# Delta rule in chunks: block-diagonal 128-row products for the inverse's halves and the updates, keys and queries in one product of 128 columns, v turned by VectorE and ScalarE

## The chip, the cores and the metric

One core of one Trainium2 chip runs the whole program in one launch. The metric is device time in microseconds (us); lower is better. TensorE is called PE in the profile (PEld is its weight load), VectorE DVE, ScalarE ACT, GpSimd POOL, SyncE SP.

## The reference, cut to what matters

The program is two layers of a network over 4096 tokens of 256 values. The change touches one of their four parts, the gated delta rule of the first layer: 16 heads of 64 channels, and for each head a 64 x 64 state S that is carried through all 4096 tokens.

```python
def step(S, inp):
    q_t, k_t, v_t, g_t, b_t = inp
    Sk = jnp.einsum('bhkv,bhk->bhv', S, k_t)
    delta = jnp.einsum('bhv,bhk->bhkv', v_t, k_t) - jnp.einsum('bhv,bhk->bhkv', Sk, k_t)
    S = jnp.exp(g_t)[..., None, None] * S + b_t[..., None, None] * delta
    o_t = jnp.einsum('bhkv,bhk->bhv', S, q_t)
    return (S, o_t)
```

## The kernel before, in words

The stages follow one another: norm and router, projections with a short convolution (`phase_projections`), the delta rule (`phase_delta`), the experts, a second norm, and an attention of 8 heads that takes the second half of the time. Only `phase_delta` changes. All of its data are float32.

**Chunks and couples.** `phase_delta` cuts the tokens into 64 chunks of C = 64. Two chunks make a couple; there are 32 couples (L754 to L780). The 16 heads are NPAIR = 8 pairs: the two heads of a pair lie on partitions 0 to 63 and 64 to 127, so every tile is 128 partitions x 8 pairs x 64. Within a chunk the recurrence becomes matrix work: a 64 x 64 triangular matrix of each head (`upper`, from keys times keys, decays and beta) is inverted by doubling, and the inverse times a residual gives the updates `u`, which go into the outputs and the new state.

**Quarter products.** Every product of a pair and head is a matmul of 64 rows, 64 weight columns and 64 moving columns (`product`, L835), so each uses one quarter of the 128 x 128 array. SAME writes the half of the partitions from which it reads, OTHER the other half. `over_heads` (L976) issues 16 of them (8 pairs, 2 heads), or 32 when a SAME and an OTHER product go side by side; I call such an issue a **group**. The trace shows every float32 matmul as two records on PE and two weight loads on PEld.

**The inverse.** Levels k = 1 to 5 each do, for both chunks x of the couple: `half` (L905, `pd_pre` <- `inv_low`, `upper`) on TensorE, `mask_step` (L1251, `step`) on VectorE, `up` (L916, `pd_low` <- `inv`, `step`) on TensorE, `turn_low` (L1262, `inv_low`) on VectorE and `keep_inverse` (L1159, `inv`) on ScalarE, and after level 5 `keep_last_inverse` (L1165, `inv_fin`). Halves and ups are SAME.

**The rest of a couple**, for each x: keys with keys (`keys_keys`, L863), keys with queries (L877), keys by rows (L888), v by rows (`values`, L897: a product with minus the identity that starts the sum of the residual), residual (L923), old outputs (L933), updates (L944), new outputs (L951), new state (L962), and a projection of both chunks' outputs in two parts (`project`, L965, 128 rows by 64 columns, L972). ScalarE copies the residual out of PSUM (L1154).

**Order.** `couples(one)` (L774) writes the program of each engine out in full, without a loop, 34 times: `one(post, pre, ahead)` weaves three couples: `post` runs the recurrent part, `pre` is inverted, `ahead` has its keys and decays prepared. The order in each engine's `one` is by hand (TensorE L986, ScalarE L1176, VectorE L1266, GpSimd L1378, loads on SP L796), and semaphores tie them. On TensorE a couple is 26 steps: 24 groups and the projection's two parts.

Of the kernel before, what the change touches and what calls it, by code (L numbers as in the profile page):

```python
# [49 lines left out]
def shape_constants():  # L50
# [14 lines left out]
    for n in range(LEVELS):  # L65
# [7 lines left out]
        "less_eye": -eye_c,  # L73
# [609 lines left out]
def phase_delta(nc, g, ctx):  # L683
# [5 lines left out]
    def ps(name):  # L689
        return ctx.enter_context(nc.psum_tensor(name, [P, NPAIR, C], F32))  # L690
# [7 lines left out]
    def sem2(name):  # L698
# [7 lines left out]
    k_t, q_t, v_t = (sb(n, [P, 2, NPAIR, 2, C]) for n in ("k_t", "q_t", "v_t"))  # L706
# [3 lines left out]
    grow = sb("grow", [P, 4, NPAIR, C + 1])  # L710
    rel = sb("rel", [P, 4, NPAIR, C + 1])
    upper = sb("upper", [P, 4, NPAIR, C])
    k_g = sb("k_g", [P, 2, NPAIR, C])
# [5 lines left out]
    inv_fin = [sb(f"inv_fin{x}", W) for x in range(2)]  # L719
# [5 lines left out]
    o_t = sb("o_t", [P, 2, NPAIR, C])  # L725
# [5 lines left out]
    p_r, p_o, p_u, p_n = ps("pd_r"), ps("pd_o"), ps("pd_u"), ps("pd_n")  # L731
# [6 lines left out]
    val_d, res_d, ress_d, w_d, u_d, o_d, ocp_d = (sem(s) for s in ("val", "res", "ress", "w", "u", "o", "ocp"))  # L738
# [3 lines left out]
    kk_d, qk_d, kr_d, rows_d, upper_d, minus_d, att_d, inv1_d = (  # L742
        sem2(s) for s in ("kk", "qk", "kr", "rows", "upper", "minus", "att", "inv1"))
# [8 lines left out]

    SAME, OTHER = range(2)

# [28 lines left out]
    def _(sp):  # L783
# [12 lines left out]
        def one(post, pre, ahead):  # L796
# [10 lines left out]
            load("k", k_t, ahead).then_inc(k_in[ahead.odd], 16)  # L807
            if ahead.c == 0:
                sp.dma_start(wo[:], g.given["wo_t"].rearrange("(n p) d -> p n d", p=P)).then_inc(wo_in, 16)
# [4 lines left out]
            if ahead.c > 1:  # L814
                sp.wait_ge(val_d, ahead.ended[1] - 4)
# [4 lines left out]
            if ahead.c > 1:  # L820
                sp.wait_ge(o_d, ahead.ended[1] - 4)
            load("q", q_t, ahead).then_inc(q_in[ahead.odd], 16)
# [6 lines left out]
    def _(pe):  # L829
        te = nc.tensor  # L830

        def rows_of(half):
            return slice(half * C, (half + 1) * C)

        def product(p, h, out, to, lhs, rhs, start=True, stop=True, shared=False):  # L835
            return te.matmul(out[rows_of(h if to == SAME else 1 - h), p, :], lhs(p, rows_of(h)), rhs(p, rows_of(h)), start=start, stop=stop,  # L836
                             skip_group_check=shared)
# [12 lines left out]
        def wait_keys(n, x):  # L850
            pe.wait_ge(k_in[n.odd], n.filled)
            if x == 0:
                if n.c > 1:
                    pe.wait_ge(ress_d, n.ended[1] - 4)
                elif n.c > 0:
                    pe.wait_ge(upper_d[0], n.last)
            else:
                if n.c > 1:
                    pe.wait_ge(state_d, n.ended[1] - 3)
                if n.c > 0:  # L860
                    pe.wait_ge(att_d[1], n.last)

        def keys_keys(n, x):  # L863
# [3 lines left out]
        def wait_queries(n, x):  # L867
            pe.wait_ge(q_in[n.odd], n.filled)
            if x == 0:
                pe.wait_ge(upper_d[1], n.now)  # L870
                pe.wait_ge(rows_d[1], n.last)
            else:
                pe.wait_ge(att_d[0], n.now)
                if n.c > 0:
                    pe.wait_ge(state_d, n.ended[0] - 1)

        def keys_queries(n, x):  # L877
            return lambda p, h: product(p, h, p_n, OTHER, of_couple(k_t, n.ring[x]), of_couple(q_t, n.ring[x]))

        def wait_key_rows(n, x, ahead):  # L880
            if x == 0:
                pe.wait_ge(ocp_d, n.begun[0])
            elif ahead is not None:
                pe.wait_ge(upper_d[1], ahead.now)
            else:
                pe.wait_ge(state_d, n.ended[0])

        def key_rows(n, x):  # L888
            return lambda p, h: product(p, h, p_o if x == 0 else p_n, OTHER, of_couple(k_t, n.ring[x]), of_const("eye_c"))

        def wait_values(n, x, ahead):
# [1733 lines left out]
```

## Time and profile before

| | us |
|---|---|
| median of 3 runs (lowest to highest) | 4342.76 (4340.51 to 4347.18) |
| the profiled execution, its own time | 4350.06 |
| its span, first to last instruction | 4348.3 |
| TensorE busy, whole span | 3834.0 |
| VectorE busy, whole span | 2981.2 |
| delta stage, from the 1st to the 31st of the 32 couples' ends | 619.5 to 1827.4 |

The profiled execution's own time is the one that a sum over its rows has to be held against; the median of the runs is 7.3 us below it. Busy time on TensorE counts each matmul to its modelled end, so a matmul that took 0.22 us to come out of the array counts 0.22 us even where the next one started 0.03 us after it. "Idle before <- issue" is time in which the engine stood still and no semaphore of another engine explains it.

### The profile page before, as it was taken

The numbers are of one execution on the slowest core, as the hardware profiler recorded it, in microseconds if no ns is written. First come the engines' busy times: TensorE is split into PE (matmuls) and PEld (weight loads), VectorE is DVE, ScalarE is ACT, GpSimd is POOL, SyncE is SP. The second block draws the span as 40 slices with busy tenths as digits, with TensorE's granted clock in tenths as the row PEclk, the third lists the DMA queues.
The fourth block names the chain that finished last, engine by engine and source line by source line (L and its number), as shares of the span: only waits on it lengthen the run. The fifth ranks groups of instructions, "written<-read, shape, count | busy, mean of one in ns | idle before, by whom it ended". The sixth has DMA issues, their size and how long they took to land. (4 is left out here: it accounts for less than half of the span.)

```text
span 4348.3 us, 135609 instructions
## 1 busy us (share of the span) xinstructions
PE 3834.0 (88%) x56333; PEld 2258.0 (52%) x56333; DVE 2981.2 (69%) x4999; ACT 2057.0 (47%) x2941; POOL 1035.6 (24%) x1042
## 2 busy tenths in 40 slices
PE   5999777777777777799687999999999999999998
PEld 4444366666676666667465344444444444444443
DVE  5799754444454444444797787887878787878786
ACT  2788622222222222225343365665656565656554
POOL 1000055445554545300777200000000000000000
PEclk9999899999999999999898899999999999999999
DMA  3543532222222222135344100000000000000000
GB/s 125 183 126 116 158 102 77 85 77 74 84 78 78 79 77 80 37 96 154 112 109 121 38 5 8 15 10 14 10 14 3 19 5 19 5 9 13 10 14 10
DMA packets 271832, 265.83 MB, mean 61 GB/s; under 512 B 53761, under 2 KB 232065, under 8 KB 270497
## 3 DMA queue, kind: packets, MB, share of 16 engines
q1 hardware_dynamic: 250768, 226.11, 17.4%
q0 software_dynamic: 6144, 16.79, 1.2%
q10 hardware_dynamic: 14352, 14.55, 1.0%
q8 instruction: 457, 7.49, 0.7%
q14 instruction: 111, 0.90, 0.1%
HBM read 151.99 MB, written 105.38 MB: 59 GB/s over the span
## 5 line engine op out<-in xcount | busy, mean ns | idle before, releaser
L2411 DVE TENSOR_REDUCE part_max<-p_m 128x1 f32<-128x512 f32 x2118 | 1362.9, 685 | 378.5 <-PE p_m L2253 371.0
L2393 ACT ACTIVATE prob<-p_s 128x1024 f32<-128x1024 f32 x1024 | 1048.6, 1024 | 747.4 <-PE p_s L2317 745.5
L2272 PE MATMUL p_o<-prob,v_one 128*64 128x512 f32 x4096 | 1055.0, 592 | 3.9 <-ACT prob L2393 0.5
L2253 PE MATMUL p_m<-keys,queries 96*64 96x512 f16 x4236 | 662.0, 387 | 27.9 <-DMA keys<-parts_d 20.3
L2317 PE MATMUL p_s<-queries,keys 97*64 97x512 f16 x4096 | 619.6, 380 | 0.0
L2317 PEld LDWEIGHTS p_s<-queries,keys 97*64 97x64 f16 x4096 | 229.4, 109 | 597.1 <-issue 592.0
L836 PE MATMUL pd_pre<-inv_low,upper 64*64 64x64 f32 x10240 | 386.6, 226 | 97.3 <-issue 80.4
L2221 POOL TENSOR_TENSOR attn<-o_num,o_inv 32x512 f32<-32x512 f32 x64 | 81.0, 1266 | 1458.5 <-DVE o_inv L2430 1452.0
L836 PEld LDWEIGHTS pd_pre<-inv_low,upper 64*64 64x64 f32 x10240 | 351.6, 140 | 104.3 <-issue 92.8
L2253 PEld LDWEIGHTS p_m<-keys,queries 96*64 96x64 f16 x4236 | 239.4, 108 | 309.3 <-DVE part_max L2411 56.4
L1255 DVE TENSOR_TENSOR step<-pd_pre,const 128x512 f32<-128x512 f32 x320 | 218.9, 689 | 245.5 <-PE pd_pre L836 240.3
L836 PE MATMUL pd_low<-inv,step 64*64 64x64 f32 x8192 | 313.6, 226 | 83.5 <-issue 70.1
L2272 PEld LDWEIGHTS p_o<-prob,v_one 128*64 128x64 f32 x4096 | 289.1, 136 | 162.2 <-issue 15.9
L589 PE MATMUL p_proj<-xn_t_all,proj_w_sb 128*128 128x512 f32 x768 | 337.2, 595 | 7.7 <-PEq L2556 7.7
L1264 DVE STREAM_TRANSPOSE inv_low<-pd_low 128x512 f32<-128x512 f32 x256 | 182.3, 712 | 233.1 <-PE pd_low L836 229.9
L836 PEld LDWEIGHTS pd_low<-inv,step 64*64 64x64 f32 x8192 | 284.5, 140 | 83.8 <-issue 82.0
L1163 ACT ACTIVATE inv<-pd_low 128x512 f32<-128x512 f32 x192 | 114.6, 597 | 336.4 <-DVE inv_low L1264 333.0
L589 PEld LDWEIGHTS p_proj<-xn_t_all,proj_w_sb 128*128 128x128 f32 x768 | 146.6, 191 | 192.6 <-issue 187.3
L1163 ACT ACTIVATE inv_half<-pd_low 128x512 f32<-128x512 f32 x64 | 38.3, 598 | 262.9 <-DVE inv_low L1264 262.9
L972 PE MATMUL pd_u<-wo,o_t 128*64 128x256 f32 x1024 | 138.7, 415 | 4.2 <-issue 4.2
L2430 DVE RECIPROCAL o_inv<-o_raw 128x64 f32<-128x64 f32 x256 | 137.8, 540 | 0.0
L658 DVE SCALAR_TENSOR_TENSOR conv_k<-raw,conv_w_sb,conv_k 128x2048 f32<-128x2048 f32 x48 | 112.2, 2351 | 22.9 <-ACT raw L632 21.8
(244 smaller groups left out, 5837.1 us busy)
## 6 DMA issues: line engine op xcount, KB each, us to landing
q_d<-conv_q SPq DMA_DIRECT2D x16, 1024.0 KB, 5.0
v_d<-conv_v SPq DMA_DIRECT2D x16, 1024.0 KB, 5.0
k_d<-conv_k SPq DMA_DIRECT2D x16, 1024.0 KB, 6.5
sums<-sums_d SPq DMA_DIRECT2D x128, 128.0 KB, 3.8
k_t<-k_d SPq DMA_DIRECT2D x32, 512.0 KB, 4.1
sums_k<-sums_d SPq DMA_DIRECT2D x128, 128.0 KB, 3.0
v_t<-v_d SPq DMA_DIRECT2D x32, 512.0 KB, 4.6
q_t<-q_d SPq DMA_DIRECT2D x32, 512.0 KB, 5.2
```

Source lines behind the costliest of these rows:

```text
L589: last = te.matmul(p_proj[u % RING][:], g.proj_w_sb[:, n, c, p * P:(p + 1) * P], g.xn_t[:, c, b * BLK:(b + 1) * BLK], start=c == 0, stop=c ...
L836: return te.matmul(out[rows_of(h if to == SAME else 1 - h), p, :], lhs(p, rows_of(h)), rhs(p, rows_of(h)), start=start, stop=stop, skip_gr ...
L972: last = te.matmul(out[x * C:(x + 1) * C, 0:D], o_t[:, x, p, :], wo[:, p, :], start=p == 0, stop=p == NPAIR - 1)
L1163: a.activation(inv_half[x][:] if k == NL - 1 else inv[x][:], p_low[x][:], ACT.Copy).then_inc(up_d[x], 1)
L1255: v.tensor_tensor(step[x][:], p_pre[x][:], over_pairs(masks[:, k - 1, :]), ALU.mult).then_inc(step_d[x], 1)
L1264: v.transpose(inv_low[x][:], p_low[x][:]).then_inc(lowc_d[x], 1)
L2253: last = te.matmul(p_m[k % 2][x * HALF:(x + 1) * HALF, :], queries[0:ROW, p, hh, at:at + HALF], keys[0:ROW, 2 * p + hh, kb * BLK:(kb + 1) ...
L2272: product = te.matmul(p_o[64 * hh:64 * hh + VW, :], g.v_one[:, j, p, hh:hh + 2, :].rearrange("p a d -> p (a d)"), prob[:, j % 2, hh, :], s ...
L2317: last = te.matmul(p_s[j % 2][x * HALF:(x + 1) * HALF, hh, :], keys[0:KR, 2 * p + hh, at:at + HALF], queries[0:KR, p, hh, :], start=True, ...
L2393: a.activation(prob[:, j % 2], p_s[j % 2][:], ACT.Exp, scale=SCORE_SCALE).then_inc(exp_d, 1)
L2411: v.tensor_reduce(part_max[:, hh * SUB + sub, kb:kb + 1], p_m[k % 2][:], AX.X, ALU.max).then_inc(red_d, 1)
L2430: v.reciprocal(o_inv[:, i * PW:(i + 1) * PW], o_raw[:, i * PW:(i + 1) * PW]).then_inc(inv_d, 1)
```

## The change

`half` and `updates` become matmuls of 128 rows, 128 weight columns and 64 moving columns, one for a pair instead of two for its heads. To that end `upper` is copied into a zeroed block-diagonal tile `upper_wide` (`widen`, on ScalarE), and the last inverse is copied in two halves into a zeroed block-diagonal `inv_fin`. Keys with keys and keys with queries become one product with 128 moving columns (`keys`, `pd_kq` of two banks), and q is loaded earlier. The product `values` goes: VectorE turns v in 32 x 32 blocks (`turn_values`), ScalarE puts the blocks in place by eight copies for each chunk (`keep_values`, `v_row`), and VectorE subtracts the residual product from it (`residual`), which takes ScalarE's copy of the residual away. The projection becomes 128 x 128 weights for both chunks. The order of all engines is written anew.

```diff
-    k_t, q_t, v_t = (sb(n, [P, 2, NPAIR, 2, C]) for n in ("k_t", "q_t", "v_t"))
+    kq_t = sb("kq_t", [P, 2, 2, NPAIR, 2, C])
+    k_t, q_t = kq_t[:, 0], kq_t[:, 1]
+    upper_wide = sb("upper_wide", [P, 2, NPAIR, 2 * C])
+    inv_fin = [sb(f"inv_fin{x}", [P, NPAIR, 2 * C]) for x in range(2)]
...
+        def keys(n, x):
             key = of_couple(k_t, n.ring[x])
-            return lambda p, h: product(p, h, p_r if x == 0 else p_n, OTHER, key, key)
+            return lambda p, h: product(p, h, p_kq, OTHER, key, lambda p, hs: kq_t[hs, :, n.odd, p, x, :])
...
         def half(n, x):
-            return lambda p, h: product(p, h, p_pre[x], SAME, of(upper, n.ring[x]), of(inv_low[x]))
+            for p in range(NPAIR):
+                last = te.matmul(p_pre[x][:, p, :], upper_wide[:, x, p, :], inv_low[x][:, p, :], start=True, stop=True)
+            return last
...
         def updates(n, x):
-            return lambda p, h: product(p, h, p_u, SAME, of(inv_fin[x]), of(resid))
+            for p in range(NPAIR):
+                last = te.matmul(p_u[:, p, :], inv_fin[x][:, p, :], resid[:, p, :], start=True, stop=True)
+            return last
...
             for p in pairs:
-                for x in range(2):
-                    last = te.matmul(out[x * C:(x + 1) * C, 0:D], o_t[:, x, p, :], wo[:, p, :], start=p == 0, stop=p == NPAIR - 1)
+                last = te.matmul(out[:, 0:D], o_t[:, p].rearrange("p x t -> p (x t)"), wo[:, p, :], start=p == 0, stop=p == NPAIR - 1)
...
+        def keep_values(n, x, h):
+            for from_p, from_t, to_p, to_t in blocks_of(h):
+                last = a.activation(v_row[to_p, x, :, to_t], v_turned[from_p, :, from_t], ACT.Copy)
...
+        def widen(n, x):
+            if n.c > 0:
+                act.wait_ge(half_d[x], n.level[0])
+            act.wait_ge(minus_d[x], n.now)
+            for h in range(2):
+                last = a.activation(upper_wide[half_of(h), x, :, half_of(h)], upper[x][half_of(h)], ACT.Copy)
+            last.then_inc(wide_d[x], 1)
...
+        def turn_values(n, x):
+            v.transpose(v_turned[:], v_t[:, n.odd, :, x, :]).then_inc(vt_d[x], 1)
+
+        def residual(n, x):
+            v.tensor_tensor(resid[:], v_row[:, x], p_r, ALU.subtract).then_inc(ress_d, 1)
...
+        po.memset(upper_wide[:], 0.0).then_inc(cleared, 1)
+        for x in range(2):
+            po.memset(inv_fin[x][:], 0.0).then_inc(cleared, 1)
```

TensorE's order for one couple is now, with x after the point and "+" for products side by side: residual.0 + old.0; half.0, half.1 of level 1; updates.0; up.0; up.1 + new state.0; half.0, half.1 of level 2; up.0 + residual.1; up.1 + outputs.0; half.0 of level 3; updates.1; half.1 of level 3; old.1 + new state.1; up.0 + outputs.1; up.1 + keys.0 of the next couple but one; half.0, half.1 of level 4; up.0 + key rows.0; projection, first part; up.1 + keys.1; half.0, half.1 of level 5; projection, second part; up.0 + key rows.1; up.1.

Three places show what stands on TensorE. In an order's row, "64x64" or "128x64" is output partitions by moving columns, and xN a row repeated. The first is the end of a couple, level 5 and the second part of the projection (`pd_u<-wo,o_t`), before:

```order
L836 MATMUL pd_pre<-inv_low,upper 64x64 [waits d_lowc0]
L836 MATMUL pd_pre<-inv_low,upper 64x64 x15
L836 MATMUL pd_pre<-inv_low,upper 64x64 [waits d_lowc1]
L836 MATMUL pd_pre<-inv_low,upper 64x64 x15
L972 MATMUL pd_u<-wo,o_t 64x256 x8
```

and in the changed kernel:

```order
L901 MATMUL pd_pre<-inv_low,upper_wide 128x64 [waits d_lowc0]
L901 MATMUL pd_pre<-inv_low,upper_wide 128x64 x7
L901 MATMUL pd_pre<-inv_low,upper_wide 128x64 [waits d_lowc1]
L901 MATMUL pd_pre<-inv_low,upper_wide 128x64 x7
L977 MATMUL pd_u<-wo,o_t 128x256 x4
```

Each half has 8 matmuls instead of 16, and each part of the projection 4 instead of 8. The second is the middle of a couple, on TensorE at level 3, where the updates of chunk 1 stand, before:

```order
L836 MATMUL pd_o<-q_t,state 64x64 x15
L836 MATMUL pd_u<-resid,inv_fin 64x64 [waits d_u,d_ress,d_up1]
L836 MATMUL pd_u<-resid,inv_fin 64x64 x15
L836 MATMUL pd_pre<-inv_low,upper 64x64 [waits d_lowc0]
L836 MATMUL pd_pre<-inv_low,upper 64x64 x15
```

and in the changed kernel:

```order
L901 MATMUL pd_pre<-inv_low,upper_wide 128x64 x7
L948 MATMUL pd_u<-resid,inv_fin 128x64 [waits d_u,d_ress,d_up1]
L948 MATMUL pd_u<-resid,inv_fin 128x64 x7
L901 MATMUL pd_pre<-inv_low,upper_wide 128x64 [waits d_lowc1]
L901 MATMUL pd_pre<-inv_low,upper_wide 128x64 x7
```

The updates now stand between the two halves of level 3, and the old outputs, which stood alone in a group, have moved behind them to the side of the new state. Over the 32 couples TensorE has 14592 matmuls in this stage, before 19968: 456 for a couple instead of 624.

## Rows read from the trace of the kernel before

**Rows 1.** The page, first line and busy times: us (share of the span) x instructions.
```profile
span 4348.3 us, 135609 instructions
...
PE 3834.0 (88%) x56333; PEld 2258.0 (52%) x56333; DVE 2981.2 (69%) x4999; ACT 2057.0 (47%) x2941; POOL 1035.6 (24%) x1042
```

**Rows 2.** Windows, stretch, busy us of PE, PEld, DVE, ACT, POOL; clock, DMA share, GB/s.
```profile
1000.00:1400.00 400.00, 309.09 (x12380) 273.95 (x12380) 196.13 (x299) 105.95 (x188) 201.24 (x189) 0.96 0.25 80
```

**Rows 3.** Tile attn_tok, written once per couple: ns, first and last start.
```profile
L1204 ACT ACTIVATE attn_tok<-pd_u x31: 384/384/386, 619.5 to 1827.4; 128x256 f32<-128x256 f32 x31
```

**Rows 4.** Timeline, TensorE: start us, us, tiles, count [idle <- cause].
```profile
1199.79 0.22 PE L836 MATMUL pd_n<-q_t,k_t 64*64 64x64 f32 x1
...
1200.69 0.22 PE L836 MATMUL pd_n<-q_t,k_t 64*64 64x64 f32 x1
1200.73 1.11 PE L836 MATMUL pd_o<-q_t,state 64*64 64x64 f32 x32
1201.66 1.11 PE L836 MATMUL pd_u<-resid,inv_fin 64*64 64x64 f32 x32
...
1203.44 0.33 PE L836 MATMUL pd_pre<-inv_low,upper 64*64 64x64 f32 x5 [0.45 <-issue]
```

**Rows 5.** Waits of 1000 to 1400 us, TensorE: us in total, times, longest us.
```profile
PE pd_pre L836 <- issue: 28.8, 20, 3.2
...
PE pd_low L836 <- DVE step L1255: 2.9, 5, 0.6
```

**Rows 6.** DMA queues of 1000 to 1400 us: packets, MB, share.
```profile
q8 instruction: 98, 1.61, 1.7%
```

**Rows 7.** DMA queues of 110 to 510 us, the projections.
```profile
q8 instruction: 7, 0.11, 0.1%
```

**Rows 8.** Timeline, TensorE, half of a projection between two other groups.
```profile
1212.05 0.22 PE L836 MATMUL pd_o<-const,k_t 64*64 64x64 f32 x1
1212.19 1.95 PE L972 MATMUL pd_u<-wo,o_t 128*64 128x256 f32 x16
1214.07 0.27 PE L836 MATMUL pd_low<-inv,step 64*64 64x64 f32 x1
```

**Rows 9.** Timeline, TensorE, first group of the router product L451.
```profile
14.59 3.62 PE L451 MATMUL p_logits<-lin_w,xn_t 128*128 128x48 f32 x16 [0.87 <-ACT xn_t L401]
```

**Rows 10.** Windows over that group: stretch, busy us, clock, DMA share, GB/s.
```profile
14.60:18.10 3.50, 3.50 (x16) 3.45 (x16) 0.00 (x0) 0.67 (x3) 2.32 (x3) 1.00 1.11 338
2110.00:2112.00 2.00, 1.96 (x18) 1.76 (x16) 1.79 (x8) 0.94 (x2) 0.54 (x2) 1.00 0.00 0
```

**Rows 11.** Groups by form: transpositions by 128 columns, early and late.
```profile
L443 PE MATMUL p_xt<-const,xn 128*128 128x128 f32 x64 | 15.7, 427 | 16.6 <-DVE xn L264 16.6
...
L1826 PE MATMUL ps_xn<-const,xn 128*128 128x128 f32 x64 | 12.5, 278 | 24.5 <-DVE xn L1973 24.5
```

**Rows 12.** Timeline, TensorE, a group of L1861.
```profile
2110.01 1.95 PE L1861 MATMUL ps_qk<-z_t,qk_w 128*128 128x128 f32 x16
```

**Rows 13.** Groups by form, weight loads: busy us, mean ns.
```profile
L836 PEld LDWEIGHTS pd_pre<-inv_low,upper 64*64 64x64 f32 x10240 | 351.6, 140 | 104.3 <-issue 92.8 <-DVE inv_low L1264 6.5
...
L1861 PEld LDWEIGHTS ps_qk<-z_t,qk_w 128*128 128x128 f32 x512 | 59.8, 192 | 0.1
...
L451 PEld LDWEIGHTS p_logits<-lin_w,xn_t 128*128 128x128 f32 x128 | 27.9, 330 | 21.3 <-issue 21.3
```

**Rows 14.** Groups by form, 1000 to 1400 us: DVE and ACT.
```profile
L1255 DVE TENSOR_TENSOR step<-pd_pre,const 128x512 f32<-128x512 f32 x100 | 68.4, 688 | 80.1 <-PE pd_pre L836 78.4
L1264 DVE STREAM_TRANSPOSE inv_low<-pd_low 128x512 f32<-128x512 f32 x79 | 56.2, 712 | 75.0 <-PE pd_low L836 74.0
...
L1204 ACT ACTIVATE attn_tok<-pd_u 128x256 f32<-128x256 f32 x10 | 3.8, 384 | 29.6 <-PE pd_u L972 29.6
```

**Rows 15.** Timeline, VectorE, waiting for a product of TensorE.
```profile
1201.10 0.69 DVE L1238 TENSOR_TENSOR qk<-pd_n,rel 128x512 f32<-128x512 f32 x1 [0.38 <-PE pd_n L836]
```

**Rows 16.** Timeline, GpSimd, at the start of the delta stage.
```profile
535.56 1.83 POOL L1318 MEMSET rel<- 128x2080 f32 x1
```

More of the change, by code:

```diff
@@ L807, in one @@
             load("k", k_t, ahead).then_inc(k_in[ahead.odd], 16)
+            if ahead.c > 1:
+                for x in range(2):
+                    sp.wait_ge(kq_d[x], ahead.before)
+                    sp.wait_ge(qg_d[x], ahead.before)
+            load("q", q_t, ahead).then_inc(q_in[ahead.odd], 16)
             if ahead.c == 0:
@@ L814, in one @@
             if ahead.c > 1:
-                sp.wait_ge(val_d, ahead.ended[1] - 4)
+                for x in range(2):
+                    sp.wait_ge(vt_d[x], ahead.before)
             load("v", v_t, ahead).then_inc(v_in[ahead.odd], 16)
@@ L1080, in one @@
             if post is not None:
-                new.then_inc(new_d, 1)
+                out.then_inc(o_d, 1)
             if pre is not None:
@@ L1196, in one @@
             if post is not None:
+                keep_outputs(post, 0)
+            if pre is not None:
+                keep_inverse(pre, 0, 3)
+            if post is not None:
                 keep_outputs(post, 1)
             if pre is not None:
-                for k in (3, 4):
-                    for x in range(2):
-                        keep_inverse(pre, x, k)
+                keep_values(pre, 0, 0)
+                keep_inverse(pre, 1, 3)
+                keep_values(pre, 0, 1)
+                keep_inverse(pre, 0, 4)
+                keep_values(pre, 1, 0)
+                keep_inverse(pre, 1, 4)
+                keep_values(pre, 1, 1)
+            if ahead is not None:
+                for x in range(2):
+                    widen(ahead, x)
             if post is not None:
@@ L1266, in one @@
         def one(post, pre, ahead):
+            if post is not None:
+                residual(post, 0)
             if pre is not None:
@@ L1308, in one @@
             if ahead is not None:
+                attention(ahead, 1)
                 turn_first(ahead, 0)
+            if pre is not None:
+                take_rows(pre, 1)
+            if ahead is not None:
                 turn_first(ahead, 1)
@@ L1383, in one @@
                     decays(ahead, x)
-            if pre is not None:
-                grow_queries(pre, 0)
-                grow_keys(pre, 0)
-            if ahead is not None:
-                for x in range(2):
-                    scale_rel(ahead, x)
+                scale_rel(ahead, 0)
             if post is not None:
@@ L1396, in one @@
                 scatter(post)
+            if pre is not None:
+                grow_queries(pre, 1)
             if ahead is not None:
-                for x in range(2):
-                    minus_eye(ahead, x)
-                for x in range(2):
-                    first_inverse(ahead, x)
+                minus_eye(ahead, 0)
+                first_inverse(ahead, 0)
+                minus_eye(ahead, 1)
+                first_inverse(ahead, 1)
         couples(one)
```

359 lines of the change are left out of this document (172 added, 187 removed).

## The prediction

> **What bounds the kernel now.** The page first: TensorE is busy for 3834.0 us of 4348.3, and it is the only engine near the span [rows 1]. Then the windows, because only one stage changes. In 400 us of the delta stage TensorE is busy for 309.09 us, VectorE 196.13, ScalarE 105.95, GpSimd 201.24, at a granted clock of 0.96 [rows 2]. So TensorE leads here too, with a quarter of its time idle. The period comes from the tile that ends each couple: 31 writes, 619.5 to 1827.4 us [rows 3], 30 intervals of 40.26 us.
>
> What a group costs is in the timeline. A group of one product (32 records) starts at 1200.73 and the next at 1201.66: 0.93 us [rows 4]. A group of two products side by side, 64 records, spans 1199.79 to 1200.73 and takes no longer [rows 4]. So the price is 0.058 us for each of 16 turns, whether two or four quarters of the array work in it. The 24 groups of a couple are 22.3 us. Half a projection takes 16 records in 1.73 us (1.95 less the 0.22 until a result is out) [rows 8], two make 3.5. A change between the two tilings costs something: the last quarter matmul starts at 1212.05, the projection at 1212.19, where a quarter matmul would have followed after 0.03; I take 0.15 us for each of the four changes, 0.6. Together 26.4 us of the 40.26; TensorE stands still for nearly 14.
>
> The waits say why: "issue" ended 28.8 us of idle time before `pd_pre` alone, the VectorE step only 2.9 us before `pd_low` [rows 5]. A gap of 0.45 us stands in the middle of a group, at 1203.44, where no semaphore is asked [rows 4]. The DMA rows tell what it is: in 400 us of this stage the instruction queue brought 98 packets of 16.4 KB [rows 6], in 400 us of the projections 7 [rows 7]. TensorE ran 12380 + 12380 instructions in those 400 us [rows 2], so a packet holds 253 and one comes every 4.08 us. A couple's 624 matmuls are 2496 instructions, with some 30 waits 9.98 packets, 40.7 us: the stage moves at the pace at which TensorE's straight-line code is brought, not at the pace of the array.
>
> **The change, part by part (us per couple).**
>
> *Code.* 456 matmuls are 1824 instructions, with the waits 7.3 packets: 30.0 us at 4.08. This bound falls by 10.3.
>
> *Halves and updates.* Twelve groups of 16 records with 128 weight columns and 64 moving columns replace twelve of 32. Is the weight load the price? The nearest rows: L451 has 128 weight columns and 48 moving ones, and 16 records take 3.62 us [rows 9], (3.62 - 0.41) / 15 = 214 ns each, though 48 moving columns are fewer than here; early in the kernel everything is slow by a factor of two in spacing (the same transposition takes 427 ns there and 278 at L1826 [rows 11]), so I read it as the lower level of 1.2 GHz, against the 1.00 that the windows print for it [rows 10]. Half of 214 is 107 at 2.4 GHz. L1861, with 128 weight and 128 moving columns, takes (1.95 - 0.28) / 15 = 112 ns [rows 12]. The load's own record grows from 140 ns for 64 columns to 192 for 128, and to 330 early [rows 13], which fits a load of two cycles for a column that hides the matmul behind it. Bounds: 58 ns (a quarter matmul's turn) and 112; I take 110, next to the rows with 128 weight columns. A half is then 16 x 0.110 = 1.76 instead of 0.93, and it is alone, since the whole array is taken. Ten halves 17.6, two updates 3.5. The Trainium skill has the rule in "TensorE: Matmul & The Clock Gate", section "LDWEIGHTS (loading the stationary operand)": the time goes with the columns of the weights alone, columns / 1.2 ns. This gives 107 ns at either clock; the rows agree at the higher level and have twice that early. By it twelve groups would cost 0.6 less and the forecast would be 4365.
>
> *Keys and queries.* Two products of 128 moving columns, each beside an up: 16 x 0.110 = 1.76, two are 3.5. Key rows go beside ups.
>
> *The other groups* (two old outputs, two residuals, two outputs, two new states, ten ups, two key rows; two of the ups are with the keys above): ten groups of 0.93, 9.3.
>
> *Projection.* 16 records of 256 columns, 216 ns each (1.73 / 8, where two went side by side [rows 8]): 3.5, as before.
>
> *Changes of tiling.* Twelve instead of four, at 0.17 (0.14 seen, and a first load that is now longer): 2.0. Bounds 0.1 and 0.3. The Trainium skill, "TensorEngine Tiling (Array Packing)", "Key Properties", says that a change of tiling mode drains TensorE. Read strictly, each would cost the full 0.22 us of a result and the load, 0.3: 1.6 more for a couple, 4434 in all; the 0.14 us row speaks for a partial drain.
>
> Sum: 17.6 + 3.5 + 3.5 + 9.3 + 3.5 + 2.0 = 39.4, before 26.4. The array's work now exceeds the code's 30.0 and becomes the bound.
>
> *Waits that stay.* A mask takes 0.69, a turn 0.71 [rows 14], and VectorE starts 0.15 to 0.2 after the product's end [rows 15]: from the end of a group to the start of what needs it is 1.1 us. A half of 1.76 covers that, an up of 0.93 and a change nearly: 0.1 each for the exposed ones, some at the state (keys.0 waits for the state behind one group) and at old.0 (behind key rows.1), 1.1 in all. Code still stalls where 128 records are dense (outputs.0; old.1 to outputs.1; key rows.1 to residual.0): 253 instructions pass in 2 to 2.9 us there and wait for up to 1.5, but only if a packet begins there, 0.9 on average. Sum 2.0; bounds 0.5 and 9.2, all of what TensorE is idle now by its busy time ((400 - 309.09) / 9.93 couples [rows 2]), stalls for code among it. A couple: 41.4, that is +1.15.
>
> *Other engines.* VectorE gets four operations more, 34 x 0.69 = 23.5. ScalarE: 16 small copies of 32 x 256, priced at 0.384 by `attn_tok` of the same length [rows 14], 6.1; eight half copies at 0.6 in the place of two, two residuals less: about 20. GpSimd keeps its 20. All lie under 41 and their order meets TensorE's: `keep_values` ends before its level's inverse is read, `widen` 3 us before its half. Cover if it is gone: `widen` costs 1.2 a chunk. Loads: q goes ahead of `sums_k` on SP, with two couples' time in hand; nothing.
>
> *The ends of the stage.* GpSimd clears 7216 columns instead of 4160 before its first work, at 1.83 / 2080 [rows 16]: +2.7. The first inversion has no recurrent part that shares groups: ten halves, ten ups, two of them with keys, +3.
>
> Total: 31 x 1.15 + 5.7 = +41. Against the profiled execution's 4350.1 that is 4391. The median of the runs is 7.3 lower: **4384 us**, 0.95% slower. The case in one line: stalls for code are traded for weight loads of 128 columns, which cost more.
>
> **Rivals.**
>
> *A. The load does not set the pace.* If 128-column loads hide like 64-column ones, a half takes 0.93, the array has 29.5, and code at 30.0 bounds; with 2 of waits 32 us, -8.3 x 31 + 6, less the 7.3: 4092. For it: no row shows 64 moving columns with 128 weight columns at 2.4 GHz. Against: L451's 214 ns with 48. It decides below 0.10 us a record. Chance 0.10.
>
> *B. Faster by a little: the stalls go wholly.* Loads at 107 ns, changes at 0.1, waits 1.2: 17.1 + 3.4 + 3.4 + 9.3 + 3.5 + 1.2 + 1.2 = 39.1, -1.2 x 31 + 6, less the 7.3: 4312. Place: the long halves drain the queue slowly enough for the next packet to land. It decides when tiling changes, waits and stalls together are under 2.9. For it: the named waits on VectorE are small now [rows 5], and half the groups will last 1.76. Chance 0.17.
>
> *C. More waits stay.* If half of the present idle 9.2 remains, 4.6, since ScalarE and VectorE get more work and `upper` and `grow` a single buffer: 39.4 + 4.6 = 44.0, +3.7 x 31 + 6, less the 7.3: 4464. Against: both engines were half idle. Chance 0.15.
>
> *D. No change:* the new and old bounds within 0.2%, 0.08.
>
> **How the numbers follow.** Forecast 0.50, A 0.10, B 0.17, C 0.15, D 0.08. 0.2% (8.7 us) is about what a measurement of this kernel tells from no change. Faster A + B = 0.27, same 0.08, slower 0.65. The range 4290 to 4460 holds the forecast, B, D and the lower half of C; A, the upper half of C and tails of 0.03 are outside, 0.2.
>
> **What would show it.** Right: records of the half spaced about 0.11 us; instruction packets every 5.5 to 6 us; a period of about 41.4; `issue` no longer leading TensorE's idle time; a busy share of TensorE over 0.9. Wrong: spacing under 0.08 (A); a period under 40 with spacing 0.11 (B); TensorE waiting for `upper_wide`, `resid` or `inv_low` by over 3 us a couple (C). The other stages must keep their length within 2 us.

## The result, and the profile after

The changed kernel takes 4400.31 us (median of 4 runs, 4398.0 to 4403.65), the kernel before 4344.97 us on the same chip: ratio 1.0129, 95% interval 1.0111 to 1.0147. It is slower by 1.3%, on the side that was forecast and inside the range of 4290 to 4460; the forecast was 4384 us. The profiled execution took 4403.65 us.

The page's first lines, as [rows 1]:

```profile
span 4401.8 us, 115094 instructions
...
PE 4160.9 (95%) x45581; PEld 2616.3 (59%) x45581; DVE 3069.3 (70%) x5127; ACT 2350.5 (53%) x3581; POOL 1041.0 (24%) x1045
```

The same 400 us of the delta stage in the windows, as [rows 2], and the instruction queue in them, as [rows 6]:

```profile
1000.00:1400.00 400.00, 391.06 (x8727) 368.27 (x8727) 214.61 (x325) 189.50 (x369) 196.80 (x185) 1.00 0.24 76
```

```profile
q8 instruction: 69, 1.13, 1.2%
```

The tile that ends a couple, as [rows 3]:

```profile
L1204 ACT ACTIVATE attn_tok<-pd_u x32: 383/383/385, 625.7 to 1899.5; 128x256 f32<-128x256 f32 x32
```

This row has all 32 couples, so its last start is that of couple 32.

There are 30% fewer matmuls in the window, and TensorE is busy for 391 of 400 us instead of 309. Packets of code (the instruction queue's, 16.4 KB each) come every 5.8 us instead of 4.08.

TensorE's timeline shows what a full product costs:

```profile
1254.53 0.22 PE L853 MATMUL pd_kq<-state,k_g 64*64 64x64 f32 x1
1254.68 3.79 PE L901 MATMUL pd_pre<-inv_low,upper_wide 128*128 128x64 f32 x32
1258.30 1.95 PE L948 MATMUL pd_u<-resid,inv_fin 128*128 128x64 f32 x16
1260.18 0.33 PE L853 MATMUL pd_low<-inv,step 64*64 64x64 f32 x4
```

Two halves take 1258.30 - 1254.68 = 3.62 us, 1.81 each, the updates 1.88, where a quarter group takes 0.93 [rows 4]. One record follows another after (3.79 - 0.28) / 31 = 0.113 us. The change of tiling at 1254.53 takes 0.15, from that last quarter record's start to the next record's. Groups by form, weight loads and what the other engines were given (busy us, mean ns):

```profile
L901 PEld LDWEIGHTS pd_pre<-inv_low,upper_wide 128*128 128x128 f32 x1535 | 176.1, 192 | 5.7 <-issue 3.7
...
L1140 ACT ACTIVATE v_row<-v_turned 32x256 f32<-32x256 f32 x144 | 59.6, 414 | 7.3 <-DVE v_turned L1236 5.3
L1149 ACT ACTIVATE upper_wide<-upper 64x512 f32<-64x512 f32 x40 | 25.2, 629 | 0.7
```

The waits of TensorE, as [rows 5]:

```profile
PE pd_low L853 <- issue: 5.1, 13, 0.9
...
PE pd_pre L901 <- issue: 0.2, 1, 0.2
```

The 28.8 us of "issue" ahead of `pd_pre` are 0.2 now. Who waits is VectorE, for TensorE:

```profile
DVE step L1267 <- PE pd_pre L901: 92.5, 96, 1.2
```

**Where the 53.5 us of span came in.** The starts of `attn_tok` of couples 1, 31 and 32 are 619.51, 1827.36, 1845.89 before and 625.72, 1874.43, 1899.46 after. So 6.2 us are lost by the first couple's end, 40.9 in 30 intervals (40.26 to 41.62 us, +1.36 each), 6.5 in the last couple. All later stages start 53 us later and keep their length (first `p_m` 2379.9 and 2432.9).

**A couple, split.** For all kernels below I split the interval of 30 couples by the starts of TensorE's matmuls, from couple 1's end to couple 31's. Two starts over 0.33 us apart are a standstill (a change of tiling or a projection's record stays under that); "rest" is all else: the array's own pace, changes, short waits, and what a lower clock costs. Of the standstill, two columns show the single stops of over 0.45 us that nothing but "issue" explains: those that end 1.15 to 1.65 us after a packet of the instruction queue has landed ("after a packet"), and all others. "Lower clock" is the time at the lower of the granted clock's two levels. All are us per couple; "packets" counts those of the instruction queue. The periods are those of one profiled execution each. The times come from several chips, on which the kernel before took 4338 to 4352 us, so kernels are compared by their ratios.

| kernel | period | standstill | after a packet | other issue | rest | packets | lower clock | time, ratio to before (95%) |
|---|---|---|---|---|---|---|---|---|
| before | 40.26 | 11.9 | 9.9 | 0.2 | 28.4 | 9.9 | 3.2 | 1 |
| after | 41.62 | 1.4 | 0.5 | 0.1 | 40.2 | 7.2 | 0.2 | 1.0129 (1.0111 to 1.0147) |
| e1 quarter halves | 37.37 | 5.0 | 2.0 | 1.6 | 32.4 | 8.5 | 1.8 | 4265.7, 0.9804 (0.9787 to 0.9822) |
| e2 half the weight columns | 35.90 | 2.8 | 0.4 | 1.5 | 33.1 | 7.2 | 0.8 | 4218.4, 0.9698 (0.9676 to 0.9721) |
| e3 before, v by rows | 39.62 | 11.2 | 6.2 | 1.8 | 28.4 | 9.4 | 2.6 | 4329.2, 0.9948 (0.9932 to 0.9963) |
| e4 full at levels 1, 3, 5 | 39.92 | 2.4 | 0.8 | 0.5 | 37.5 | 7.7 | 1.6 | 4349.4, 0.9992 (0.9980 to 1.0005) |
| e5 quarter updates | 40.99 | 2.1 | 0.3 | 0.9 | 38.9 | 7.5 | 0.0 | 4387.3, 1.0092 (1.0068 to 1.0117) |
| e6 all quarters | 38.13 | 7.7 | 4.4 | 1.6 | 30.5 | 8.7 | 3.3 | 4287.8, 0.9852 (0.9826 to 0.9878) |
| e7 full at level 1 | 38.10 | 4.0 | 1.2 | 1.4 | 34.1 | 8.2 | 1.8 | 4295.2, 0.9872 (0.9849 to 0.9896) |
| e8 full at level 5 | 39.37 | 5.0 | 2.4 | 1.5 | 34.4 | 8.2 | 1.9 | 4315.7, 0.9913 (0.9889 to 0.9937) |
| e9 after, 160 waits | 42.05 | 1.7 | 0.3 | 0.5 | 40.4 | 7.5 | 0.3 | 4416.5, 1.0153 (1.0131 to 1.0175) |
| e10 e1, 160 waits | 37.76 | 5.2 | 2.7 | 1.2 | 32.5 | 8.5 | 1.9 | 4286.0, 0.9862 (0.9839 to 0.9885) |
| e11 e3, full updates | 40.17 | 9.4 | 5.8 | 1.0 | 30.8 | 9.1 | 3.5 | 4346.7, 0.9982 (0.9965 to 0.9998) |
| e12 e1, no widening | 36.37 | 4.5 | 3.1 | 0.1 | 31.9 | 8.5 | 0.7 | 4233.9, 0.9744 (0.9717 to 0.9771) |

The change took 10.5 us of standstill away and added 11.8 of rest. Some expectations quote periods of the middle 24 couples, which differ by up to 0.3 us (e1 37.45, e3 39.8, before 40.57).

**The stops are of two kinds.** In the kernel before, 209 of 212 such stops end 1.15 to 1.65 us after a packet has landed, where 12% of points in time taken at random do. This ties its standstill to the code, more firmly than the name "issue" does. In e1 only 48 of 129 do. Of its other 81, 77 end within 3 us after the start of one of GpSimd's two indirect DMAs of a couple (`slots_d<-rows,place`); such stretches are 12% of the time. They look like this, beside TensorE's stops at 1198.88, 1199.63 and 1200.40 (shown at e12):

```profile
1197.57 1.00 POOL L1408 DMA_INDIRECT slots_d<-rows,place  x1 [0.28 <-POOL place L1405]
...
1198.88 0.97 POOL L1408 DMA_INDIRECT slots_d<-rows,place  x1 [0.30 <-issue]
```

No run moves or removes these DMAs, so that they cause the stops is not shown. The kernel before and e12 have the same two and next to no such stops.

**The clock.** The granted clock has two levels, printed as 1.00 and 0.50. A couple of the kernel before spends 3.2 us at the lower one, a changed one 0.2. In couples wholly at the higher level the period is 39.15 us before (11 of 30 couples) and 41.51 after (29 of 30): 2.4 us apart instead of 1.36. About 1 us of what the change costs a couple is thus given back by the clock, as an estimate; such couples also have fewer stops, so it is rough.

### The profile page after: what moved, and what is told of

Its sections match the earlier page's. It is cut to its first block and busy times, and to the rows that moved or that the text cites. A ratio compares the mean times of both kernels' runs of the same rounds, so it can differ in the third digit from the quotient of the medians.

```text
span 4401.8 us, 115094 instructions
## 1 busy us (share of the span) xinstructions
PE 4160.9 (95%) x45581; PEld 2616.3 (59%) x45581; DVE 3069.3 (70%) x5127; ACT 2350.5 (53%) x3581; POOL 1041.0 (24%) x1045
## 5 line engine op out<-in xcount | busy, mean ns | idle before, releaser
L901 PE MATMUL pd_pre<-inv_low,upper_wide 128*128 128x64 f32 x5120 | 614.3, 278 | 2.6 <-DVE inv_low L1272 2.1
L901 PEld LDWEIGHTS pd_pre<-inv_low,upper_wide 128*128 128x128 f32 x5120 | 589.4, 193 | 20.6 <-issue 14.1
L853 PE MATMUL pd_low<-inv,step 64*64 64x64 f32 x8192 | 325.7, 225 | 16.7 <-issue 12.7
L1140 ACT ACTIVATE v_row<-v_turned 32x256 f32<-32x256 f32 x512 | 211.9, 414 | 25.8 <-DVE v_turned L1236 18.9
L853 PE MATMUL pd_kq<-kq_t 64*64 64x128 f32 x2048 | 133.4, 278 | 33.6 <-DMA kq_t<-q_d 30.2
L853 PEld LDWEIGHTS pd_kq<-kq_t 64*64 64x64 f32 x2048 | 115.2, 136 | 36.0 <-issue 36.0
```

What stands on the lines that cost most here:

```text
L853: return te.matmul(out[half_of(h if to == SAME else 1 - h), p, :], lhs(p, half_of(h)), rhs(p, half_of(h)), start=start, stop=stop, skip_gr ...
L901: last = te.matmul(p_pre[x][:, p, :], upper_wide[:, x, p, :], inv_low[x][:, p, :], start=True, stop=True)
L1140: last = a.activation(v_row[to_p, x, :, to_t], v_turned[from_p, :, from_t], ACT.Copy)
```

## The experiments

**e1: the ten halves as quarter products again**, from the diagonal blocks of `upper_wide`; all else as changed.

```diff
         def halves(n, x, k):
             wait_half(n, x, k)
-            half(n, x).then_inc(half_d[x], 1)
+            over_heads(half_quarters(n, x))[0].then_inc(half_d[x], 1)
```

> The changed kernel, with only the ten halves of a couple made again as quarter products (16 matmuls of 64 x 64 weights, read from the diagonal blocks of upper_wide). Theory (128-column weight loads are now the bound): the array's work falls from 39.4 us a couple by ten times 0.83 and some 0.7 of tiling changes to 30.4; the code rises from 7.3 to 8.6 instruction packets, 35.1 us at 4.08, and becomes the bound again; period 35.5 to 37 us, whole kernel 4230 to 4260 us, faster than before and than the change. Rival (the added copies and turns on ScalarE and VectorE, or the new order, cost the time): they all stay, so the period stays at 41 to 42 us and the kernel near 4400.

Measured: 4265.7 us, 37.37 a couple, 4.25 less than changed. The full halves are the loss; the rest of the change is a gain of 2.9 us. The same window:

```profile
1000.00:1400.00 400.00, 360.82 (x11464) 329.20 (x11456) 236.47 (x362) 209.56 (x413) 214.75 (x201) 0.98 0.26 84
```

ScalarE does more than in the changed kernel (209.56 us, it has more couples in the window), and TensorE is quicker, so ScalarE's new copies are not the cause of these 4.25 us. But I had expected a little less time: of the 7.8 us of rest that went, 3.5 came back as standstill, 1.5 of it after packets, 1.5 in the other stops, the rest mostly in waits for VectorE. Its waits:

```profile
PE pd_o L853 <- issue: 10.7, 14, 2.0
PE pd_kq L853 <- issue: 9.1, 23, 0.4
...
PE pd_pre L992 <- issue: 6.8, 9, 1.0
```

**e2: halves with 64 of the 128 weight columns.** It leaves out the second head of each pair in the halves, so it has as many instructions as the changed kernel and differs in weight columns alone.

```diff
-                last = te.matmul(p_pre[x][:, p, :], upper_wide[:, x, p, :], inv_low[x][:, p, :], start=True, stop=True)
+                last = te.matmul(p_pre[x][0:C, p, :], upper_wide[:, x, p, 0:C], inv_low[x][:, p, :], start=True, stop=True)
```

> The changed kernel, with each matmul of a half given only 64 of the 128 weight columns, so that only one head of each pair gets its half (this leaves out the other head's product). The number of instructions and the moving columns stay. Theory (the time goes with the weight columns): records 0.055 to 0.06 us apart, a half 0.93 instead of 1.8 us, period 32 to 34 us, kernel 4110 to 4170 us. Rival (the time goes with the whole array being taken, or with the moving columns and the mode): records stay 0.11 us apart, period near 41.6.

Measured: 4218.4 us, 35.90 a couple. Timeline:

```profile
1210.67 1.85 PE L901 MATMUL pd_pre<-inv_low,upper_wide 128*64 128x64 f32 x28 [0.33 <-issue]
```

(1.85 - 0.27) / 27 = 0.059 us a record against 0.113 with 128 columns, same rows and same moving columns. So the weights' columns set the pace, shown directly. (With half the weight columns go half the output partitions; that can't be told apart here.) The price was 5.7 us for ten halves, less than the 8 or so that I had expected, and the time is above the expected 4110 to 4170: 7.0 of rest went, 1.3 of standstill returned, all of it in stops that follow no packet.

**e3: the kernel before with v by rows alone** (`turn_values`, `keep_values`, the subtraction on VectorE; `values` and ScalarE's residual copy go; the order of TensorE stays).

```diff
-                wait_values(post, 1, None)
-                new, kept = over_heads(updates(post, 0), values(post, 1))
+                over_heads(updates(post, 0))[0].then_inc(w_d, 1)
...
-                raised, kept = over_heads(up(pre, 1, 4), values(pre, 0))
+                over_heads(up(pre, 1, 4))[0].then_inc(upmm_d[1], 1)
```

> The kernel before, with only the v part of the change: v turned by VectorE and ScalarE, the residual subtracted by VectorE, the 32 matmuls of values gone (both groups stood beside a SAME product, so the array's groups keep their length). Theory (before, the pace is that of the code): 128 instructions fewer are 0.51 packets, -2.1 us a couple, kernel about 4280 us (4265 to 4300). Rival (before, the pace is that of the groups and waits): no change, 4345 within 8, or slower by VectorE's four more operations.

Measured: 4329.2 us, 39.62 a couple, a smaller gain than the expected 4265 to 4300. Both products stood beside others, so the array's rest is unchanged (28.4), and half a packet of code went. The stops after a packet fell by 3.7 us, more than the 2.1 of the code theory, but the period by only 0.64, a third of it, because other stops came in their place: 1.6 us of "other issue" and 1.3 of waits for VectorE:

```profile
PE pd_pre L849 <- DVE inv_low L1288: 6.0, 10, 0.6
...
PE pd_pre L849 <- DVE state L1273: 4.4, 7, 0.7
```

The first is in no wait list of the kernel before, the second was 2.3 us there. So the code theory has the direction, and time gained from the code is soon bounded by something else. "Packets times 4.08" is no law, only how this kernel happened to stand (4.23 us a packet in e3).

**e4: full halves at levels 1, 3 and 5**, quarter halves at 2 and 4.

```diff
+            if k in (1, 3, 5):
+                half(n, x).then_inc(half_d[x], 1)
+            else:
+                over_heads(half_quarters(n, x))[0].then_inc(half_d[x], 1)
```

> The changed kernel, with block-diagonal halves at levels 1, 3 and 5, where they stand next to updates or projection, and quarter products at levels 2 and 4. Theory: array 39.4 - 4 x 0.83 - 0.7 = 35.4 us, code 7.3 + 4 x 0.127 = 7.9 packets, 32.1 us; the array bounds, with 1.5 of waits 36 to 37.5 us a couple, kernel 4240 to 4280 us. Rival as in the run with quarter halves: 4400.

Measured: 4349.4 us, 39.92, a miss. I had hoped that six full halves would take the standstill and cost the array little. They took 2.6 of e1's 5.0 and cost 5.1.

**e5: the changed kernel with quarter updates.**

```diff
-            for p in range(NPAIR):
-                last = te.matmul(p_u[:, p, :], inv_fin[x][:, p, :], resid[:, p, :], start=True, stop=True)
-            return last
+            return over_heads(lambda p, h: te.matmul(p_u[half_of(h), p, :], inv_fin[x][half_of(h), p, half_of(h)], resid[half_of(h), p, :],
+                                                     start=True, stop=True))[0]
```

> The changed kernel with its two updates alone back as quarter products (64 rows by 64 weight columns, read from the diagonal blocks of inv_fin); the ten halves stay 128 rows. Theory (with the halves full the array sets the period, so its price shows nearly whole): 2 x (1.79 - 0.93) = 1.7 us less for a couple, 0.3 less for changes of tiling that go, and a little code, 64 matmuls more are 1 packet for each second couple: period 39.6 to 40.4 against 41.6, time 4335 to 4365. Rival (the couple is a chain of waits and the updates lie beside them): period 41.3 or more, 4390 or more.

Measured: 4387.3 us, 40.99, 0.6 less and between the two theories: 1.3 of rest went, 0.7 of standstill came, none of it after a packet.

**e6: halves and updates as quarters** (e1 and e5 together).

> Halves and updates both as quarter products, so that only keys with queries in one product, v by rows, the projection and the new order are left of the change. Theory (with few 128-column weights the pace of the code is what holds, so the same edit of the updates now brings little): 8.9 packets for a couple, period 37.2 to 38.0 against 37.6 with full updates, time 4250 to 4280. Rival (the array holds there too): another 2.0 less, period 35.6, about 4205.

Measured: 4287.8 us, 38.13, slightly above what the theory gave. Set beside e1, the array has 1.9 us less to do and the couple takes 0.8 us longer. What came is 2.7 us of standstill, and 2.4 of it are stops after a packet; the other stops are as in e1. It stands ahead of the updates (1.2 us a couple) and, more than in e1 (5.9 and 6.8 us in this window), ahead of `pd_low` and `pd_pre`:

```profile
PE pd_low L853 <- issue: 15.2, 28, 1.8
PE pd_u L947 <- issue: 12.4, 6, 2.8
PE pd_pre L991 <- issue: 12.1, 12, 1.7
```

In e1 no such wait ahead of `pd_u` is in the list. So full updates in place of quarter ones take 0.8 us off with quarter halves around them, and add 0.6 with full halves (e5). A rival for a part of the 0.8 is the clock: e6 spends 3.3 us of a couple at the lower level, e1 1.8. In couples wholly at the higher one e6 is still 0.6 us longer (37.12 against 36.51), about as much as these two means are uncertain (0.5), while its standstill is 2.7 more there too.

**e9 and e10: 160 waits more a couple**, on a semaphore satisfied from the start, in the halves of the changed kernel and of e1.

```diff
             for p in range(NPAIR):
+                for _ in range(2):
+                    pe.wait_ge(g.const_in, 16)
                 last = te.matmul(p_pre[x][:, p, :], upper_wide[:, x, p, :], inv_low[x][:, p, :], start=True, stop=True)
```

> The changed kernel with 160 waits more for a couple, on a semaphore that was satisfied at the start, two ahead of each of the 80 matmuls of the halves. They cost the array nothing and are 160 instructions of code, 0.63 of a packet. Theory (the array holds in the full halves, code only between them): under 0.6 us for a couple, time within 20 us of the changed kernel's. Rival (the pace of the code or of the sequencer holds): 0.63 x 4.08 = 2.6 us a couple, 4480.

> The same 160 waits in the kernel with quarter halves and full updates (4265.7 us, 37.6 a couple), one ahead of each of the 160 matmuls. Theory (code holds there): 0.63 of a packet at 4.08 to 4.4 us, 2.6 to 2.8 us a couple, period 40.2, time 4340 to 4355. Rival (array or engines hold): under 0.6 us a couple, below 4285.

Measured: e9 4416.5 us, +0.4 a couple, with 7.5 packets instead of 7.2; e10 4286.0 us, +0.4, with 8.5 packets as without. The packets tell that one wait ahead of a matmul travels with it and only the second one is an instruction. So e10 added no code and can't test what it was made for; that it takes longer than e1 all the same (ratios 0.9862 and 0.9804, intervals apart) neither theory had, and it stays open. e9 added half of what I had meant and, as the theory had it, cost little: its interval overlaps the changed kernel's. The pair is inconclusive.

**e7 and e8: e1 with full halves at level 1 only, and at level 5 only** (as e4, with `(1,)` and `(5,)`).

> The kernel with quarter halves and full updates (period 37.45), with the two halves of level 1 full; they stand behind key rows.1 + up, up.1 and residual + old outputs, 320 records and over one packet and a half of dense code. Each full half adds 0.86 us of array and takes 32 instructions away, 0.125 packet. Theory (a full half pays where the code that comes next is late, as the full updates do): period 37.0 to 37.6, 4250 to 4270. Rival (a full half costs 0.4 us wherever it stands, as three levels and five levels together did): period 38.2, 4290.

> The same with the halves of level 5 full, between up.1 + keys.1 and the second part of the projection, where the projection's few instructions already give the code time. Theory (it depends on the place, and here there is nothing to hide): period 38.2 to 38.8, 4290 to 4310. Rival (0.4 us each, any place): 38.2, 4290, and no difference from level 1.

Measured: 38.10 and 39.37 a couple, 4295.2 and 4315.7 us. My theory missed both sizes: I had thought level 1 free. The rival's 38.2 us and 4290 hit level 1, and it missed level 5. That the place matters holds, with the same instructions and the same 1.7 to 2.0 us of rest: all four runs of e8 are above all four of e7. By how much is less sure. In the profiled executions level 1 took 1.0 us of standstill away and level 5 none, 1.27 us a couple apart; but the one of e7 is its fastest (4284.1) and the one of e8 its slowest (4329.0), and the medians are 20.5 us apart, 0.66 a couple. At level 5 the standstill only moved (e8's waits):

```profile
PE pd_pre L992 <- issue: 9.8, 12, 2.4
```

**e11: e3 with full updates**, in the order of the kernel before.

```diff
-                over_heads(updates(post, 0))[0].then_inc(w_d, 1)
+                updates(post, 0).then_inc(w_d, 1)
...
-            a.activation(inv_fin[x][:], p_low[x][:], ACT.Copy).then_inc(up_d[x], 1)
+            for h in range(2):
+                half_p = slice(h * C, (h + 1) * C)
+                last = a.activation(inv_fin[x][half_p, :, half_p], p_low[x][half_p], ACT.Copy)
```

> The kernel before with v by rows (period 39.8) and, added to it, the two updates as block-diagonal products of 128 rows, nothing else of the change. Adds 2 x 0.86 us of array and four changes of tiling, 2.3 us; takes 64 instructions away, 0.25 packet. Theory (the code's arrival sets the pace there): 0 to 1.0 us less, period 38.8 to 39.8, 4290 to 4330. Rival (array): +2.0, period 41.8, 4390.

Measured: 4346.7 us, 40.17: 0.55 more than e3. 2.4 us of rest were added and 1.8 of standstill went, near the code theory (gain 0 to 1.0) and far from the array's (+2.0), and in neither. Of a couple, e11 spends 3.5 us at the lower clock, e3 2.6. In couples wholly at the higher one e11 is the shorter (37.56 against 38.44, each uncertain by 0.3 to 0.5), so the 0.55 may be the clock's.

**e12: e1 without `widen`.** Quarter halves don't need the block-diagonal tile, so they read `upper`, which has its ring of four again.

```diff
-    upper = [sb(f"upper{x}", W) for x in range(2)]
-    upper_wide = sb("upper_wide", [P, 2, NPAIR, 2 * C])
+    upper = sb("upper", [P, 4, NPAIR, C])
...
-            return lambda p, h: te.matmul(p_pre[x][half_of(h), p, :], upper_wide[half_of(h), x, p, half_of(h)], inv_low[x][half_of(h), p, :],
+            return lambda p, h: te.matmul(p_pre[x][half_of(h), p, :], upper[half_of(h), n.ring[x], p, :], inv_low[x][half_of(h), p, :],
...
+            if n.c > 1:
+                pool.wait_ge(half_d[x], n.level[0] - NL)
```

> The best version so far (quarter halves, full updates, keys with queries in one product, v by rows; 37.45 us a couple, 4265.7 us) without widen: the halves read upper itself, which gets its ring of four buffers back, so ScalarE loses four copies of 64 x 512 a couple, 4 x 0.629 = 2.5 us of its 20, and GpSimd a memset. Nothing changes on TensorE but an address. Theory (ScalarE's and VectorE's added work lies beside TensorE's and costs nothing): period 37.2 to 37.7, time 4255 to 4275. Rival (ScalarE's added work delays what TensorE waits for and is part of the loss): 1 us or more less for a couple, below 4240.

Measured: 4233.9 us, 36.37 a couple, the fastest version that computes everything: 2.6% under the kernel before and 3.8% under the changed one (0.9744 / 1.0129). The 1.0 us a couple under e1 is what the rival had said. Its mechanism isn't shown, though. The same window:

```profile
1000.00:1400.00 400.00, 364.25 (x11854) 333.68 (x11843) 244.97 (x375) 191.80 (x385) 223.99 (x210) 0.99 0.27 87
```

Spread over the tiles, 1.85 us of a couple went at old outputs + new state of chunk 1, where nothing of `widen` is awaited, and 0.9 came elsewhere. In e1 that group stops several times in its middle, by "issue" (timeline):

```profile
1198.88 0.21 PE L853 MATMUL pd_kq<-u,k_row 64*64 64x64 f32 x1 [0.38 <-issue]
...
1199.63 0.21 PE L853 MATMUL pd_kq<-u,k_row 64*64 64x64 f32 x1 [0.41 <-issue]
...
1200.40 0.25 PE L853 MATMUL pd_o<-q_g,state 64*64 64x64 f32 x1 [0.41 <-issue]
```

In e12's couple that I looked at it runs through, and one stop of 2.05 us comes in the next group. TensorE's instructions are the same in both. Two things differ by more than the period does. The stops of e1's kind are gone (0.1 us instead of 1.6), though GpSimd's indirect DMAs stand beside the same groups, and stops after a packet came for them (3.1 instead of 2.0). And the clock is higher: 0.7 us of a couple at the lower level instead of 1.8. In couples wholly at the higher one, e12 takes 36.14 us (27 of 30) and e1 36.51 (19 of 30), 0.4 apart and within their scatter. So more than half of the gain may be the clock's, and no wait for ScalarE's copies is seen; what set off the difference stays open.

## Why the prediction was right, step by step

**What bound the kernel before.** "The stage moves at the pace at which TensorE's straight-line code is brought": 11.9 us of standstill, of which 9.9 end just behind a packet's landing, e3's gain with the array's work unchanged, and e6 against e1, where 64 instructions more brought 2.4 us more of such stops, support it. Too simple was the bound "packets by 4.08": over all kernels a packet takes 4.08 to 5.75 us. I had "code 30.0" and "array 39.4" as two bounds, of which the larger counts. The table says that they add up in part: where records are dense the array waits, where they are wide it doesn't, and one doesn't pay for the other. The estimate that TensorE stands still for nearly 14 us was 2 too high: the other 2 are in "rest", with the short waits and the time at the lower clock.

**Halves and updates, the term that decides.** Taken 0.110 us a record, measured 0.112 to 0.113; a half 1.76 against 1.81. At the lower clock level the same records are 0.213 to 0.214 apart (21 such steps in the changed kernel, 143 in e4), as L451's were; so the reading of that early row as the lower level is borne out, against the 1.00 printed for it. That rival A falls is shown twice, by the changed kernel's spacing and by e2. The Trainium skill, "TensorE: Matmul & The Clock Gate", section "LDWEIGHTS (loading the stationary operand)", gives columns / 1.2 ns, 107 for 128 columns and 53 for 64; the records have 112 to 113 and 58 to 59, so at the higher level it holds here within 5 and 10%. At the lower level the trace has twice its figure, so that "at either clock" in the prediction is wrong for this kernel.

**Changes of tiling.** Taken 0.17 for each; seen 0.15 to 0.2 into the whole array, and 0.2 to 0.3 out of it, whose first load is longer. The strict reading of "TensorEngine Tiling (Array Packing)" in the Trainium skill, a full drain at each change, isn't borne out on the way in: 0.15 is less than the 0.22 of one result, as the profile models its end.

**Sum and waits.** 39.4 + 2.0 = 41.4 against 40.2 + 1.4 = 41.6. The rest is 0.8 above my array sum, which had the exposed short waits in the other term. That the errors of the two terms cancel to 0.2 is partly luck. So is that no term for the clock was needed: all prices were from rows at the higher level, and only the result shows that the changed stage stays there. Rivals B and C are out by the period: 39.1 and 44.0.

**Other engines: nothing.** VectorE waits for TensorE for 92.5 us of 400 at the mask alone. e1 keeps all of ScalarE's and VectorE's work in a faster kernel, so it lies beside TensorE's; in the changed kernel no wait for ScalarE shows among TensorE's. Only e12 leaves a doubt, of up to 1 us and of 0.4 at the higher clock level. A copy of 32 x 256 takes 0.414 us, priced at 0.384.

**The ends of the stage** were mis-sized, and the errors partly cancel. GpSimd's clearing, "+2.7", cost nothing: before, GpSimd waited 1.37 us there for a load; now it begins 1.2 us sooner and is done at 538.9, and the first decays began at 538.85, before at 538.77. The first couple, "+3", cost 6.2; e1, with quarter halves, ends it at 619.8, so this goes with the ten full halves, which have no recurrent part beside them. The three kernels that have all ten end it at 625.7 to 632.5 and the others at 612.5 to 620.3; e5, with less wide work than the changed kernel, has the 632.5, so a single first couple varies by several us. The last couple, which I left out, cost 6.5. TensorE's windows there, changed kernel first, then the kernel before:

```profile
1874.40:1879.00 4.60, 3.53 (x163) 3.31 (x164) 1.38 (x2) 2.75 (x5) 0.00 (x0) 1.00 0.01 4
1879.00:1884.00 5.00, 3.59 (x47) 3.29 (x46) 1.02 (x2) 0.00 (x0) 0.00 (x0) 0.70 0.00 0
1884.00:1889.00 5.00, 4.54 (x73) 4.50 (x74) 1.04 (x2) 0.60 (x1) 3.17 (x4) 0.62 0.11 44
1889.00:1894.00 5.00, 3.87 (x91) 3.58 (x92) 1.38 (x2) 0.00 (x0) 0.00 (x0) 0.72 0.04 15
```

```profile
1832.00:1837.00 5.00, 3.08 (x106) 2.91 (x102) 1.38 (x2) 0.60 (x1) 0.91 (x1) 1.00 0.01 3
1837.00:1842.00 5.00, 3.99 (x136) 3.78 (x130) 0.69 (x1) 1.19 (x2) 2.26 (x4) 1.00 0.16 56
```

The clock was granted at 0.62 to 0.72 where it was 1.00 before, and the chain of lone groups ran slower. The wide products are not the main cause: e6, which has none of them, takes 23.7 us for this couple, the kernel before 18.5 and the changed one 25.0:

```profile
1763.80:1787.40 23.60, 17.56 (x432) 15.24 (x428) 4.83 (x7) 3.88 (x8) 3.17 (x4) 0.86 0.04 13
```

So 5.1 of the 6.5 us come with the rest of the change.

The account: 30 x 1.36 + 6.2 + 6.5 = 53.5 of span, where I had 31 x 1.15 + 5.7 = 41. Both parts were too low by about 6 us: the period by 0.2 us a couple, and the ends, where the last couple was put at one period's difference.

**What the forecast didn't see** is that the same change holds a gain. Its last line, "stalls for code are traded for weight loads of 128 columns", is true of the halves: ten of them add 7.8 us of rest, and e1 has only 5.0 of standstill for them to remove. They could not have paid, whatever the code did. (With stops counted from 0.25 us on, it is 8.3 against 7.1, and the same holds.) For the two updates it went either way: a gain of 0.8 us in e1's surroundings, a loss of 0.6 beside full halves. Keys with queries, v by rows, the projection and the new order were worth 2.1 us a couple together (before against e6); which of these isn't told apart, except that v by rows alone was worth 0.64 in the kernel before (e3).

## What to carry to other kernels

Fewer, larger matmuls save instructions, but when weights double their columns the array pays the load; count how much standstill there is to win before paying, because that is the most that can come back. A bound by code and a bound by the array don't take turns over a whole period: judge each group by what stands next to it. Wide products paid between dense groups as the updates in e1, not at levels 1 and 5 (e7, e8), so try the place before relying on it. An edit that frees TensorE can bring more stops for code than it saves (e6). Test "issue" against the landing of code packets before calling it code, and read the granted clock of each kernel before explaining 1 us of a couple.

## What the runs showed of the hardware that I had not expected

- Instruction packets never came closely: the shortest distance is 3.2 to 3.6 us in every kernel here, at 253 of TensorE's recorded instructions each. Yet a kernel with a packet every 4.3 us stands still for 4.5 us of a couple (e12).
- "Issue" has two kinds. One is a stop that ends 1.15 to 1.65 us after a packet of code has landed (209 of 212 in the kernel before). The other is a row of stops of 0.6 us between starts inside a group (e1 at 1198 to 1201 us); 77 of 81 of these in e1 end within 3 us after the start of an indirect DMA of GpSimd. Why, and why not in every kernel, is not shown.
- The granted clock in the window rose from 0.96 to 1.00 when the busy share rose from 77 to 98%, and in the last couple it fell to 0.62 (such values are means over the two levels, 1.00 and 0.50). I had put no term for either. At the lower level, records with 128 weight columns are 0.213 to 0.214 us apart instead of 0.112.
- One wait ahead of a matmul adds no instruction to the stream; a second one does (8.5 packets in e10 and in e1, 7.5 in e9 and 7.2 in the changed kernel).
